# A fused transformer block on one core: head fillers as plain products, and a sum over weight halves in narrower pieces

## What is computed

```python
x = x + layernorm(attn_ref(layernorm(x), ...))
x = x + layernorm(ffn_ref(layernorm(x), ...))

# attn_ref
n  = ln(x, ln_g, ln_b)
W1 = gelu(n @ h1_w1 + h1_b1) @ h1_w2 + h1_b2        # 128 -> 512 -> 128
W2 = gelu(n @ h2_w1 + h2_b1) @ h2_w2 + h2_b2
W3 = tril(einsum('bzn,bsn->bzs', W1, W2))
t  = ln(gelu(einsum('bzs,bsm->bzm', W3, n)), ln_g, ln_b)
out = x + mlp(ln(x + t, ln_g, ln_b), fm_w1, fm_b1, fm_w2, fm_b2)

# ffn_ref: weights are -1, 0 or 1 with a scale by row
h = silu(x @ w1) * (x @ w2)
h = gelu(h @ h1); h = gelu(h @ h2)                   # 512 -> 512
out = h @ w3
```

## Time and profile before

| | |
|---|---|
| median of 3 runs | 372.45 us (372.44 to 372.49) |
| the profiled execution | 374.7 us |
| its span, first to last instruction | 373.0 us |
| mean granted clock of TensorE | 0.986 of full |
| busy in it | PE 357.8, DVE 334.7, ACT 302.9, POOL 134.0 us |

### The profile page before, as it was taken

The page is one execution under the profiler, slowest core; times in us unless marked ns, Lnnn a source line. Parts: engine busy times, 40 slices in busy tenths (PEclk is TensorE's granted clock), DMA queues, the critical chain, the costliest instruction groups (busy, mean ns, idle before and its releaser), DMA issues.

```text
span 373.0 us, 6094 instructions
## 1 busy us (share of the span) xinstructions
PE 357.8 (96%) x1812; PEld 295.0 (79%) x1812; DVE 334.7 (90%) x999; ACT 302.9 (81%) x540; POOL 134.0 (36%) x197
## 2 busy tenths in 40 slices
PE   7999899999999999999999999999999999999991
PEld 6787687768877888878888887788877888878991
DVE  5999988999999999999988998787998999987754
ACT  5999869786799877996959689977989578959890
POOL 4332971691164036322531174003750163032221
PEclk9999969999999999999999999999999999999997
DMA  7743000000000000100000000000000001000111
GB/s 232 244 130 102 0 2 1 1 2 0 4 0 0 2 1 0 31 0 3 0 0 2 2 28 2 0 0 3 30 28 2 0 3 28 3 0 1 30 29 32
DMA packets 8404, 9.08 MB, mean 24 GB/s; under 512 B 561, under 2 KB 6194, under 8 KB 8370
## 3 DMA queue, kind: packets, MB, share of 16 engines
q1 hardware_dynamic: 7826, 8.41, 7.5%
q10 hardware_dynamic: 544, 0.26, 0.2%
HBM read 6.57 MB, written 2.10 MB: 23 GB/s over the span
## 4 chain that ended last, share of the span: by engine, by line
PE 62%; DVE 20%; ACT 7%; issue 5%; POOL 3%; DMA 1%; SPq 1%; POOLq 0%; DVEq 0%; ACTq 0%
PE bank L1214 8%; PE bank L1216 8%; PE bank L1230 6%; PE bank L1231 6%; PE bank L1118 4%; PE bank L1115 3%; PE bank L1116 3%; PE bank L1099 3%; PE bank L1196 3%; PE bank L1199 3%; PE bank L1103 3%; PE bank L1100 3%; PE bank L1142 3%; PE bank L1041 2%; DVE h_hidden_lo L690 2%
## 5 line engine op out<-in xcount | busy, mean ns | idle before, releaser
L690 DVE TENSOR_TENSOR ffn_gate_lo<-bank,ffn_gate_hi 128x512 fp32r<-128x512 f32 (+1 forms) x72 | 44.3, 622 | 7.9 <-ACT bank L560 5.8
L488 ACT ACTIVATE h_hidden_hi<-bank,cols 128x512 fp32r<-128x512 f32 x64 | 43.7, 701 | 4.6 <-PE bank L1103 4.2
L690 DVE TENSOR_TENSOR h_hidden_lo<-bank,h_hidden_hi 128x512 fp32r<-128x512 f32 x64 | 42.5, 676 | 2.6 <-ACT bank L493 2.6
L560 ACT ACTIVATE bank<-bank,cols 128x512 f32<-128x512 f32 (+1 forms) x72 | 43.7, 623 | 0.5
L493 ACT ACTIVATE bank<-bank,cols 128x512 f32<-128x512 f32 x64 | 42.2, 679 | 0.6
L1214 PE MATMUL bank<-ffn_gate_hi,ffn_w_hi 128*128 128x512 f32 (+1 forms) x108 | 40.0, 377 | 0.0
L1216 PE MATMUL bank<-ffn_gate_lo,ffn_w_hi 128*128 128x512 f32 (+1 forms) x108 | 39.3, 370 | 0.0
L554 ACT ACTIVATE ffn_h_hi<-bank,cols 128x512 fp32r<-128x512 f32 (+1 forms) x36 | 22.8, 644 | 10.6 <-PE bank L1216 8.6
L545 ACT ACTIVATE ffn_gate_hi<-bank 128x512 fp32r<-128x512 f32 (+1 forms) x36 | 19.5, 557 | 10.0 <-DVE bank L899 9.3
L1099 PE MATMUL bank<-aT_hi,attn_w_lo 128*128 128x512 f32 x64 | 26.2, 409 | 1.0 <-DVE h_hidden_lo L690 0.9
L538 ACT ACTIVATE raw<-bank,gate_half 128x512 f32<-128x512 f32 (+1 forms) x36 | 23.4, 657 | 4.7 <-PE bank L1199 3.8
(11 more groups left out here) (163 smaller groups left out, 1123.9 us busy)
## 6 DMA issues: line engine op xcount, KB each, us to landing
raw<-ffn_w SPq DMA_DIRECT2D x5, 512.0 KB, 3.6
out<-X SPq DMA_DIRECT2D x7, 256.0 KB, 2.3
raw<-attn_w SPq DMA_DIRECT2D x6, 256.0 KB, 4.8
X<-x SPq DMA_DIRECT2D x2, 256.0 KB, 5.5
raw<-ffn_w SPq DMA_DIRECT2D x1, 256.0 KB, 3.6
X<-x SPq DMA_DIRECT2D x1, 128.0 KB, 2.4
X<-x ACTq DMA_DIRECT2D x1, 128.0 KB, 2.7
out<-X SPq DMA_DIRECT2D x1, 128.0 KB, 1.9
```

The lines of the kernel that those rows point to most:

```text
L488: nc.scalar.activation(dst, bank(f"{L}u{j}", c)[:, :], ACT.Gelu, bias=bias_of(L, j)).then_inc(*hi[L].done(c, j))
L560: nc.scalar.activation(u, u, ACT.Gelu, scale=cols[:, C_HS[L] + j:C_HS[L] + j + 1]).then_inc(*act2[L].done(c, j))
L690: return nc.vector.tensor_tensor(dst, whole, high.bitcast(f32), ALU.subtract)
```

## The change

Three edits. The fillers are plain f32 products of ident with itself, 4, 5 and 2 of them, where 6, 16 and 8 transposes stood. The low halves are added 256 columns at a time, in 22 adds where 11 stood, and lo_acc is half as wide. b2_row has no memory of its own and lies in the first row of M, which is first written by m_norm(0). No step changes its place.

```diff
--- before.py
+++ after.py
@@ -128,14 +128,14 @@
         neg_half, zeros = sb("neg_half", [P, T]), sb("zeros", [P, T])
         ones = sb("ones", [P, 1])
         lo_ends, lo_any = sb("lo_ends", [P, FP + 1]), sb("lo_any", [P, FP + 1])
-        lo_acc = sb("lo_acc", [P, DI])
+        lo_acc = sb("lo_acc", [P, 2 * P])
         lo_flag = sb("lo_flag", [1, 1])
         warm = sb("warm", [P, 1])
 
-        b2_row = sb("b2_row", [1, D])
         NF, XR, XRB = sb("NF", [P, T, D]), sb("XR", [P, T, D]), sb("XRB", [P, T, D])
         n_tok = halves("n_tok", [P, T, D])
         M = sb("M", [P, T, D])
+        b2_row = M[0:1, 0, :]
         OTA = sb("OTA", [P, N])
         aT, mT, yT = halves("aT", [P, N]), halves("mT", [P, N]), halves("yT", [P, N])
         WT = {L: halves(f"{L}T", [P, N]) for L in ("h1", "h2")}
@@ -179,7 +179,7 @@
         ffn_hi, ffn_lo = steps("ffn_hi", FP), steps("ffn_lo", FP)
         fm_b, fm_b_added = steps("fm_b"), steps("fm_b_added")
         gate_consts = steps("gate_consts", 2)
-        lo_added, lo_reduced = steps("lo_added", ffn_w.shape[1] // DI), steps("lo_reduced")
+        lo_added, lo_reduced = steps("lo_added", ffn_w.shape[1] // (2 * P)), steps("lo_reduced")
         lo_tested, lo_counted, lo_flagged = (steps(s) for s in ("lo_tested", "lo_counted", "lo_flagged"))
 
         nT, mT_, oT, yT_, t_ = (steps(s) for s in ("nT", "mT", "oT", "yT", "t"))
@@ -285,7 +285,7 @@
             attn_piece(0)
             attn_piece(1)
             attn_piece(2)
-            sp.dma_start(b2_row[:, :], rows[2:3, :]).then_inc(b2_in, 16)
+            sp.dma_start(b2_row, rows[2:3, :]).then_inc(b2_in, 16)
             x_piece(1, 1, 2)
             for i in (3, 4, 5):
                 attn_piece(i)
@@ -337,8 +337,8 @@
             def lo_add(i):
                 c0, c1, _ = F_PIECES[i]
                 pool.wait_ge(*ffn_lo.at(0, i))
-                for w in range(c0, c1, DI):
-                    piece, n = Fw[1][:, w:w + DI].bitcast(f32), lo_added.count
+                for w in range(c0, c1, 2 * P):
+                    piece, n = Fw[1][:, w:w + 2 * P].bitcast(f32), lo_added.count
                     if n:
                         pool.wait_ge(*lo_added.at(0, n - 1))
                     nc.gpsimd.tensor_tensor(lo_acc[:, :], lo_acc[:, :] if n else piece, piece, ALU.add).then_inc(*lo_added.done(0, n))
@@ -1083,7 +1083,7 @@
                     w = ATTN["fmu"] + j * P
                     nc.tensor.matmul(bank("fb", 0)[:, j:j + 1], raw[:, w:w + P], cols[:, C_B:C_B + 1], start=True, stop=True)
                 pe.wait_ge(b2_in, 16)
-                last = nc.tensor.matmul(bank("fb", 0)[:, J:J + 1], b2_row[:, :], ones[0:1, :], start=True, stop=True)
+                last = nc.tensor.matmul(bank("fb", 0)[:, J:J + 1], b2_row, ones[0:1, :], start=True, stop=True)
                 last.then_inc(*fm_b.done(0))
 
             def up_mm(L, j, c):
@@ -1153,10 +1153,10 @@
 
                 bank_free(group, c)
                 for _ in range(n):
-                    nc.tensor.transpose(bank(group, c)[:, 0:P], ident[:, :], ident[:, :])
+                    nc.tensor.matmul(bank(group, c)[:, 0:P], ident[:, :], ident[:, :], start=True, stop=True)
 
             pe.wait_ge(*consts.at(0, 1))
-            fill("rb", 0, 6); make_rows(); fill("nT", 0, 16); n_transpose(0); fill("h1u0", 0, 8); up_mm("h1", 0, 0)
+            fill("rb", 0, 4); make_rows(); fill("nT", 0, 5); n_transpose(0); fill("h1u0", 0, 2); up_mm("h1", 0, 0)
             up_mm("h1", 1, 0); up_mm("h2", 0, 0); fm_bias_product(); up_mm("h1", 2, 0); up_mm("h2", 1, 0); up_mm("h1", 3, 0)
             down_mm("h1", 0, 0); up_mm("h2", 2, 0); down_mm("h1", 1, 0); up_mm("h2", 3, 0); n_transpose(1); down_mm("h1", 2, 0)
             down_mm("h1", 3, 0); down_mm("h2", 0, 0); up_mm("h1", 0, 1); down_mm("h2", 1, 0); up_mm("h1", 1, 1)
```

## The result

| | before | after |
|---|---|---|
| median of 6 runs each, side by side | 372.46 us | 374.78 us |
| lowest to highest | 372.16 to 375.39 | 373.94 to 377.06 |
| ratio, 95% interval | | 1.0070 (1.0038 to 1.0102) |

The changed kernel is slower by 2.3 us in the medians; by the interval of the ratio 1.4 to 3.8 us. The forecast was 373.4, its range 371.9 to 375.2.

The account below looks back on a forecast made before the run. The prediction took TensorE to set the end in most places, with the narrower adds on POOL the term that counts. It summed 0 + 0 + 0.45 + 0.50 = +0.95 us on 372.45 to 373.4 us, range 371.9 to 375.2.

Parts of the forecast that it names:

- forecast's own range: Whole kernel: 372.9 to 374.2 us, from 0.15 a wide add to both lags in full; chance 0.53.
- b2_row 0: b2_row in M's memory: read at about 12.2, M first written at 49.06, no wait added, 0 us.
- Fillers 0: Plain products in the head at 0.43 us each: net 0, bounds a lead of 0.32 and a loss of 1.7.
- The gain ends there: Head: aT_hi starts 0.3 us earlier, but ScalarE still waits for the weight piece landing at 9.43, so 0 gained.
- The ACT instruction at 9.43 in its place: Sign in the head: ScalarE's instruction that waits for a weight piece stays at 9.43.
- The price of an add: POOL: 0.74 us per 256-column add plus 0.08 between, so 0.27 more for each of the eleven wide adds.
- First place: Eight narrow adds ahead of x1_r(0) on POOL: x1_r(0) 1.21 us late, M done at 51.63, +0.45 passed on.
- Pays 0.87 − 0.42 = 0.45: Products before fm_hidden: TensorE's 0.87 us wait, less 0.42 as two intervals move to the high clock.
- Second place: Around the branch: four adds make y_r(0) 1.08 us later, y_norm(0), y_transpose(0) and everything behind 0.50 later.
- Cheap adds: Rival: 0.08 us more per wide add, slack hides it, no slower, 371.9 to 372.5 us; chance 0.20.
- The slow stretch goes away or moves: Rival: the 0.50-clock stretch from about 48.3 to 55.1 is removed by the change, 370.9 to 372.7 us; chance 0.15.
- The clock stays down longer: Rival: TensorE's 0.87 us idle delays the clock's rise at 55.1, up to 1.7 us lost, 375.1 us; chance 0.12.

Follow-up runs that it names:

- e8: Kernel before with only b2_row moved into M's first row: 372.97 us for 373.42, ratio 0.9983.
- e1: Kernel before with only the fillers changed to plain products, adds still wide: 373.42 us for 373.21, ratio 1.0000.
- e2: Kernel before with only the adds made 256 columns wide and lo_acc half as wide: 375.60 us for 373.21, ratio 1.0062.
- e11: Changed kernel, lo_add(1) behind x1_r(0), lo_add(2) behind n_low(2) and held until n_second(3) ends, y_r(0) ahead of o_shift_(0): 372.47 us, before 372.86.
- e4: Kernel before with 44 adds of 128 columns: 381.67 us, ratio 1.0221 to the kernel before.
- e5: Changed kernel with POOL's order x_r(1), x1_r(0), lo_add(1), n_low(2), lo_add(2): 375.55 us, before 373.42, ratio 1.0044.
- e6: Changed kernel, narrow adds, lo_add(1) behind x1_r(0) and lo_add(2) to lo_add(4) behind n_low(2): 375.82 us, ratio 1.0058 to the kernel before.
- e7: Kernel before with plain fillers, wide adds, lo_add(1) behind x1_r(0) and lo_add(2) to lo_add(4) behind n_low(2): 377.42 us, ratio 1.0093.
- e10: Kernel before, lo_add(1) behind x1_r(0), lo_add(2) behind n_low(2) and held until n_second(3) ends: 372.00 us, before 372.86, ratio 1.0000.
- e3: Changed kernel with only lo_add(1) moved behind x_r(1) and x1_r(0) in POOL's list: 375.73 us, ratio 1.0074 to the kernel before.
- e12: Kernel before, plain fillers, lo_add(1) behind x1_r(0), lo_add(2) after n_low(2) and n_second(3), y_r(0) ahead of o_shift_(0): 372.39 us, before 372.94.

## Why the prediction was right, and where it was off

- **Direction and places.** Slower was right, and so were both places on POOL: most of the loss is theirs. The measured 374.78 lies inside the range of 371.9 to 375.2 but above the forecast's own range of 372.9 to 374.2. The upper end that took it in was put there for slow heads and a longer slow stretch, and neither is what the profile of after shows. The direction was earned, the fit to the range was in part luck.
- **b2_row 0.** Right (e8).
- **Fillers 0.** Within what the medians can show (e1), but the step behind it was wrong. "The gain ends there" took the piece that lands at 9.43 for the bound. L1084 follows aT_hi by 3.1 us in every trace, so the lead of 0.32, given as a bound, is mostly kept. A product is two passes; 0.26 a pass in after's first eight, so some 0.5 a product for the 0.43 taken, and make_rows lay 0.06 later for it. n_transpose(0) from 6.46 and aT_hi at 7.77 came as written. "The ACT instruction at 9.43 in its place" did not: the piece had landed earlier.
- **The price of an add.** 0.742 for the 0.74, four in 3.18 for an expected 3.2.
- **First place, its size at POOL.** 1.21 was forecast; POOL shows 12.48 − 11.51 = 0.97, and VectorE's wait before M is 1.57 for "about 1.9". lo_add(1) grew by 0.55 up to the next instruction, as written. lo_add(0) grew by 0.43 only, since a wide add had been held for 1.1 us (2.38 for 1.29) beside VectorE's L710, and the narrow ones beside it lost less. The forecast left the 2.38 out.
- **First place, what passes on: the step that was mis-sized.** "Pays 0.87 − 0.42 = 0.45" rested on the stretch at 0.50 in the profile of before. After's trace has none. Against e1, with L1084 as the common mark (0.37 earlier in after), M is 0.57 + 0.37 = 0.94 later, and the first fm_hidden_lo 0.86 + 0.37 = 1.23 later, the rest from gate_half, which n_low(2) now holds up for longer, 0.96 for e1's 0.72, and from L710, 1.26 for 1.22. So 1.23 for 0.45. The 0.24 of gate_half also belongs to a term that the forecast put at 0, the four adds of lo_add(2) ahead of n_low(2). The forecast had read for itself that the profiled execution was 2.25 us longer than the median, named the missing stretch as a possible reason, and still priced the median with the stretch in it.
- **Second place.** 0.50 was forecast. From fm_hidden_lo to y_norm(0) it is 25.29 for e1's 24.74, 0.55, and to y_transpose(0) 27.31 for 26.85, 0.46. TensorE's wait is 0.89 for "near 0.85".
- **The sum.** 1.23 + 0.46 = 1.69, or 374.15 on the 372.46, which is also what the prediction gave for the case that neither kernel has the stretch (374.15). The measured median is 0.6 above that, within the interval. The lead in the head makes the gap wider: with 0.4 of it taken off, the traces of after and e1 account for 1.3 of the 2.3 us, just under the 1.4 at which the interval begins; the pair of e2 and e8 gives 2.0 for the adds. The rest is not placed. Of after's six executions two lie at 0.984 and 0.986 of the clock and at 375.5 and 377.1, of e2's seven four below 0.9885; of before's 94 beside the experiments 27 did, and of e11's twelve, with the same narrow adds, none. Whether narrow adds make slow stretches more frequent was not tested and stays open.
- **The rivals.** Cheap adds fell with the first row of L344. *The slow stretch goes away or moves* is what the profiled pair shows, but the change did not bring it about: before has the stretch in some executions and not in others. *The clock stays down longer* happened in e4, 10.2 us for 6.8, not in after's profile.

## What to carry to other kernels

An engine that is idle for two thirds of the time can still stand in the path: count what is queued between a small operation that someone waits for and the operation ahead of it. When such work is moved out of the way, look at what the other engine does in the new place. Here the orders that only followed the semaphores (e5, e6, e7) lost as much as they won or more, because VectorE and POOL hold each other up on SBUF. One added wait, which kept the adds off VectorE's steps with two SBUF inputs, brought back 1.9 us in the medians. And before a gain or a loss is called hidden under a slow stretch of the clock, look whether other executions have that stretch: the spans of before and of e1, which differ in their fillers alone, are 2.0 us apart, and 1.5 of it lies between L1084 and y_transpose(0), where before has the stretch and e1 has not.

## What the runs showed of the hardware that was not expected

- POOL beside VectorE, both on SBUF: four columns on VectorE (gate_half 0.16 alone) were busy for 0.44 to 0.99 beside n_low(2), and gate_coef for 0.65 beside a 256-column add and 1.21 beside a 512-column one. Four tiles of L754 took 1.13 alone, 2.29 and 2.31 beside narrow adds, 2.76 beside wide ones. The other way, an add of 1.29 took 2.38 beside L710. BATCH_NORM_STATS2 on X (L674), with one SBUF input, was not held up: 278 ns beside adds for 277. Narrower pieces make each hold-up shorter: the one thing for which they are good here.
- The granted clock fell to 0.50 in the profiles of before and e10 at 48.3 (6.8 us), at 48.6 in that of e4 (10.2 us), and later in others (58.2 in e3, 59.4 in e6, 60.0 in e7); in the rest it did not fall until the last 8 us. The same kernel has executions with it and without.
- By the clock records of the traces the granted clock in the head rose at 4.80 (after) to 7.97 (e1) with plain products, nine traces, and at 6.12 (e2) to 7.62 (e4) with transposes, five traces, 7.34 in before. When it rises did not decide the time: at 4.82 L1084 stands at 10.86 (e6), at 6.09 at 10.88 (e12).
